# Edge stages: encoding, node rows and score products of the first two batches in the staggered order of the loop

## What is computed

```
x = x + gnn0(layernorm(x), src, dst, edge_attr)
x = x + ffn0(layernorm(x))          # top 2 of 8 experts
x = x + gnn1(layernorm(x), src, dst)
x = x + ffn1(layernorm(x))          # top 1 of 8 experts, with a capacity
```

```
alpha = sum(h[src]*a_src) + sum(h[dst]*a_dst) + sum(relu(edge_attr @ edge_W.T + edge_b) * h[dst])
alpha = leaky_relu(alpha, 0.2)
attn  = exp(alpha - segment_max(alpha)[dst]) / segment_sum(...)[dst]
out   = segment_sum(h[src] * attn, dst) + bias
```

## Time and profile before

| | us |
|---|---|
| median of 3 runs | 6731.35 |
| the profiled execution | 6730.72 |
| its span, first to last instruction | 6728.6 |
| busy in the span: TensorE | 4888.9 |
| GpSimd | 3649.6 |
| VectorE | 3264.7 |
| ScalarE | 1365.0 |

### The profile page before, as it was taken

How to read it: one execution, slowest core, us unless ns; L and a number is a source line. 1 busy time by engine, 2 the same in 40 slices (tenths; PEclk the granted TensorE clock), 3 DMA queues, 4 the chain that set the end, 5 groups by cost and what they waited for, 6 DMA issues and landing times. The chain is left out here.

```text
span 6728.6 us, 99218 instructions
## 1 busy us (share of the span) xinstructions
PE 4888.9 (73%) x19729; PEld 3527.3 (52%) x19729; DVE 3264.7 (49%) x5938; ACT 1365.0 (20%) x2977; POOL 3649.6 (54%) x3708
## 2 busy tenths in 40 slices
PE   1689999999999992359999625656565655643698
PEld 0245555555555551359999514444444444433698
DVE  6556666666666666311111324444454444445244
ACT  1322222222222220112222201111011111101122
POOL 1667777777777750332222067777777777711322
PEclk9899999999999996579999858888888888875899
DMA  6555555555555546146666555555555555533455
GB/s 218 178 137 157 153 153 155 156 153 156 154 154 155 156 117 216 42 147 181 181 183 186 155 127 142 139 139 139 139 141 138 143 136 142 138 99 120 163 199 190
DMA packets 718013, 1022.24 MB, mean 152 GB/s; under 512 B 301733, under 2 KB 531561, under 8 KB 692608
## 3 DMA queue, kind: packets, MB, share of 16 engines
q0 software_dynamic: 183456, 485.95, 27.7%
q1 hardware_dynamic: 527676, 519.31, 25.3%
q10 hardware_dynamic: 6564, 14.14, 0.6%
HBM read 868.26 MB, written 153.27 MB: 152 GB/s over the span
## 5 line engine op out<-in xcount | busy, mean ns | idle before, releaser
L773 POOL DMA_INDIRECT e_rows<-sc_table,e_eidx x3224 | 3152.7, 978 | 1140.3 <-issue 974.0
L872 PE MATMUL e_ps_o<-e_rows,e_oh 128*128 128x264 f32 x6448 | 1665.2, 403 | 288.8 <-ACT e_res L963 147.6
L872 PEld LDWEIGHTS e_ps_o<-e_rows,e_oh 128*128 128x128 f32 x6448 | 1214.2, 196 | 747.8 <-issue 573.1
L1126 DVE TENSOR_TENSOR e_rows<-e_rows,e_ps_w 128x1024 f32<-128x1024 f32 x806 | 970.2, 1206 | 7.8 <-ACT e_rows L956 3.5
L1058 DVE SCALAR_TENSOR_TENSOR e_u<-e_encr,e_adst,e_ps_hd 128x512 f32<-128x512 f32 x806 | 593.3, 744 | 659.2 <-PE e_ps_X L822 467.4
L822 PE MATMUL e_ps_X<-e_u,e_hwide 128*104 128x512 f32 x1612 | 812.7, 597 | 16.4 <-DVE e_u L1058 16.2
L963 ACT COPY e_res<-e_ps_o 32x264 f32<-32x264 f32 x806 | 296.2, 367 | 2483.5 <-PE e_ps_o L876 2057.7
L1670 PE MATMUL x_ps_h<-x_xT,x_w 128*128 128x256 f32 x2624 | 647.3, 405 | 13.9 <-DMA x_b<-in_L_ffn_b_dram 13.9
L1670 PEld LDWEIGHTS x_ps_h<-x_xT,x_w 128*128 128x128 f32 x2624 | 638.0, 337 | 18.6 <-issue 14.8
L1681 PE MATMUL x_ps_y<-x_w,x_hT 128*128 128x256 f32 x2624 | 579.9, 379 | 0.0
L936 ACT ACTIVATE e_encr<-e_ps_enc 128x512 f32<-128x512 f32 x806 | 475.9, 590 | 370.2 <-PE e_ps_enc L810 369.4
(11 more groups left out here) (290 smaller groups left out, 4057.6 us busy)
## 6 DMA issues: line engine op xcount, KB each, us to landing
x_w<-in_L_ffn_W_dram SPq DMA_DIRECT2D x112, 1024.0 KB
e_at<-sc_grp SPq DMA_DIRECT2D x403, 192.0 KB
x_w<-in_L_ffn_w_dram SPq DMA_DIRECT2D x60, 1024.0 KB
e_rows<-sc_table,e_eidx POOLq DMA_INDIRECT x3224
e_at<-sc_grp SPq DMA_DIRECT2D x403, 96.0 KB
sc_agg<-e_res SPq DMA_DIRECT2D x816, 33.0 KB
sc_xb<-r_zero SPq DMA_DIRECT2D x24, 1032.0 KB
x_xin<-sc_xb SPq DMA_DIRECT2D x86, 258.0 KB
```

The lines of the kernel that those rows point to most:

```text
L773: pool.indirect_dma_start(rows[:, k, s, j, :], None, dr["table"][:, :], bass.IndirectOffsetOnAxis(eidx[:, k, s, j:j + 1], 0)).then_inc(s_r ...
L872: nc.tensor.matmul(ps_o[:, 0:ROW], oh[:, k, at_j:at_j + P], rows[:, k, s, j, :], start=(j == 0), stop=False)
L1126: nc.vector.tensor_tensor(part, part, ps_w[:, k, :, s * HEADS:(s + 1) * HEADS].unsqueeze(3).to_broadcast([P, CH, HEADS, DH]), ALU.mult).th ...
```

## The change

On TensorE, `scores(b, s)` is replaced by `products(b)`, which goes through all 13 sub-batches of batch 0 or 1. In layer 0 it issues E(s,0), S(s-2,0), E(s,1), S(s-2,1), and the last four scores at the end; the wait for `u` ahead of a score goes, except for those last four (the encoding's own wait for `u` of s-1 covers it). In layer 1 it issues `score_owner(b, s-2)`, and the last two at the end. The wait for the score tile, `free_scores`, stands at s = 2. On VectorE the one-hot of s+1 is made before the products of s, not after them.

```
-            def scores(b, s):
-                if s == 0:
-                    free_scores(b)
-                if not first:
-                    score_owner(b, s)
-                    return
-                enc(b, s, 0)
-                enc(b, s, 1)
-                score(b, s, 0, True)
-                score(b, s, 1, True)
+            def products(b):
+                for s in range(SB):
+                    if s == 2:
+                        free_scores(b)
+                    if first:
+                        for h in range(2):
+                            enc(b, s, h)
+                            if s >= 2:
+                                score(b, s - 2, h, False)
+                    elif s >= 2:
+                        score_owner(b, s - 2)
+                if first:
+                    for s in range(SB - 2, SB):
+                        score(b, s, 0, True)
+                        score(b, s, 1, True)
+                else:
+                    score_owner(b, SB - 2)
+                    score_owner(b, SB - 1)
...
-            for s in range(SB):
-                scores(0, s)
+            products(0)
...
-            for s in range(SB):
-                scores(1, s)
+            products(1)
...
             for s in range(SB):
+                if s + 1 < SB:
+                    owners(0, 0, s + 1, (s + 1) % 2)
                 if first:
                     products(0, s, s % 2)
-                if s + 1 < SB:
-                    owners(0, 0, s + 1, (s + 1) % 2)
...
             for s in range(SB):
+                if s + 1 < SB:
+                    owners(1, 1, s + 1, (SB + s + 1) % 2)
                 if first:
                     products(1, s, (SB + s) % 2)
-                if s + 1 < SB:
-                    owners(1, 1, s + 1, (SB + s + 1) % 2)
```

## The result

The changed kernel takes 6696.77 us (median of 6 runs, 6693.58 to 6697.89); the kernel before, in 6 runs too, 6730.57 us. The ratio is 0.9951 [0.9938, 0.9964], a gain of 33.8 us. The forecast was 6697. The mechanism was right, but some of the terms were off by 2 to 4 us and cancel, so the hit to the microsecond is luck.

What follows compares the result with a forecast made beforehand. A TensorE chain bounds batches 0 and 1, GpSimd's gathers second; TensorE bounds the loop. Gain 35.6 at batch 1's logits less 1.8 for the clock is 33.8 us: 6696.9 from the profiled 6730.72, plus 0.6 for the median, 6697; range 6690 to 6711.

Steps and rivals of the forecast that it cites:

- The cycle: Layer 0, batches 0 and 1: a staggered sub-batch takes 2.58 us, set by TensorE, against 4.52; ReLU and VectorE stay under.
- A cold start of 7.4 us: Start of batches 0 and 1: TensorE's clock rises 7.4 us after the first matmul; a batch takes 38.4 us.
- The gathers end batch 0: Batch 0's logits wait for the 52nd gather, at 313.26 instead of 327.24: 13.98 us earlier.
- the 6.3 us of cover: Batch 0: TensorE's scores end 6.3 us ahead of need, as the logits wait for gathers.
- A slowdown of the gathers: Denser VectorE work could slow GpSimd's gather issue; taken as nothing, upper end 5 us at 1.30 per gather.
- Gather 104 and logits(1): Batch 1's logits wait for its last gather until 378.6, not 414.17; gain 35.6 us, TensorE standing still 4.2.
- The clock after that wait: After TensorE's 4.2 us stall at batch 1's logits, half clock costs 3.7 us or nothing; middle of 1.8 taken.
- Loads: VectorE's new wait for the next group's load has 1.1 us of slack; cost taken as nothing, DMA share about 0.75.
- rival 1: Loads pace the sub-batches of batches 0 and 1 at 3.4 us; gain 28.1, time 6703; 14%.
- Batch 2: GpSimd restarts at 376.3, 31.9 us earlier; its 52nd gather fits by 1.0 us; 0 to 3 may be lost, none taken.
- rival 2: The loop gives back 15 to 20 us through TensorE waits for gathers; 10 to 20 stay, time 6711 to 6721; 7%.
- Rivals 3 and 4: Batches 0 and 1: clock stays at half, 6747 us, 3%; or an overlooked wait keeps the 4.5 us cycle, 6731, 3%.

Runs made afterwards that it cites:

- the busier start: Changed kernel plus one extra 400-column matmul after each encoding of sub-batches 0 and 1 in batches 0 and 1 of layer 0; 7840.15 us, one run.
- the replaced gathers: Changed kernel with layer 0's gathers of batches 0 and 1 replaced by plain copies of the table's first rows; 6709.52 against 6735.45 us, 0.996.
- the run meant to part the two: Changed kernel with VectorE's one-hots of batch 0 held back until the gathered logits are copied; 7844.19 against 7875.9 us, 0.9962.

## Why the prediction was right, step by step

**The cycle**, forecast 2.58: 2.65. Of the other bounds that the step had listed, ReLU and VectorE's work stayed under it. The 0.07 comes to 0.8 us over eleven sub-batches; its cause isn't shown.

**A cold start of 7.4 us**: mis-sized. The step took the time to the rise from before, where TensorE's first sub-batches had scores in them. Staggered, sub-batches 0 and 1 have none, and the clock rose after 11.7 and 9.6 us, about 276.5 and 338.0. That is some 2 and 1 us per batch; the busier start, in its one run, and the rises of the other traces point to the sparse work. Forecast 38.4 per batch, measured 41.3 and 40.9.

**The gathers end batch 0**: right in kind, and the 6.3 us of cover took in batch 0's longer run. The 52nd was due at 307.71 less the 1.1 of the stage's start, 306.6, and came at 308.22: one issue took 2.41 us instead of 0.95. It stands beside VectorE's 1.89 us `e_oh`, as in five more kernels here. In the kernel before, the gather beside `e_oh` was the 67th, so it cost the logits of batch 0 nothing. A slowdown of the gathers, a term put at nothing, was thus 1.6 us. Nor is `e_oh` alone in this: the longest issue among batch 1's gathers lies beside a scan, which also reads two operands from SBUF, the memory of the engines. The timeline of the kernel after:

```profile
315.55 1.23 DVE L1090 TENSOR_TENSOR_SCAN e_fmax<-e_fr,e_lk 104x512 f32<-104x512 bf16 x1
...
315.72 1.80 POOL L773 DMA_INDIRECT e_rows<-sc_table,e_eidx  x1 [0.30 <-issue]
```

All six issues among the changed kernel's 104 that took over 1.06 us began while a VectorE operation of that kind ran, as the six long ones of the kernel before did. Then 2.94 to the copy and 0.68 to TensorE, as forecast. The delay that the forecast had weighed, by the Trainium skill's rule on tensor_scalar (SBUF — State Buffer, Who interferes with whom), would have come from the owner compares: the gathers beside these took at most 1.06 us, so the trace doesn't bear it out for them. Batch 1 begins 12.3 us earlier against the stage's start; the forecast had 13.98.

**Gather 104 and logits(1)**: against the stage's start the gather came 1.7 us later than before, the long issue again, and the copy came 3.98 us after it, not 2.87. The window 376 to 378 has a DMA share of 0.83 at 195 GB/s; that this traffic is the reason isn't shown. TensorE, itself 3.1 us later at the first aggregation than forecast, waited 2.83 (1.07 of it usual), not 4.2 more than usual. Forecast 378.6, measured 380.28, 33.9 earlier than before and 32.8 against the stage's start, where the forecast had 35.6.

**The clock after that wait**: of the two ends, the costly one. It fell at about 379 and was back at about 385.7, some 6.8 us at half speed, of which TensorE worked 5.4; eight aggregation matmuls took 3.73 us instead of 1.94. That is about 2.7 us where the middle of 1.8 stood, and the trace agrees with the Trainium skill's rule (TensorE: Matmul & The Clock Gate, HAM oscillation) there, though the wait was shorter than forecast. The period from the copy of batch 1 to that of batch 2 is 72.5 us, against 69.9: 2.6 us lost. But the forecast had looked only at gaps of that size and counted one fall. The trace of before has 16 more in the loop, each around the once-a-batch logits with their usual wait of 1.07 us. The timeline and the window of before at one of them:

```profile
699.79 1.82 PE L844 MATMUL e_ps_X<-e_ident,e_alog 128*104 128x128 f32 x8 [1.07 <-ACT e_alog L940]
701.41 2.93 PE L872 MATMUL e_ps_o<-e_rows,e_oh 128*128 128x264 f32 x8
```

```profile
700.00:702.00 2.00, 2.00 (x10) 1.90 (x10) 0.34 (x1) 0.26 (x1) 1.57 (x2) 0.50 0.60 121
```

**Loads and rival 1**: 0.65 us, once, where nothing was taken. VectorE waited for a load twice ahead of the first encoding and twice in batch 1, where one half of a sub-batch took 352.73 - 350.77 = 1.96 us instead of 1.30. With the cycle's 0.8 and the start's 1.1 this makes up batch 1's 40.9. DMA share rose to 0.69, not 0.75. It takes the crowd of the replaced gathers to make the rival come true.

**Batch 2 and rival 2**: GpSimd restarts at 376.87, its 32 us gap gone, and ScalarE's copy at 452.07 waits for no gather. No stall was added in the loop. The loop in fact ended 35.0 us early where it began 31.3 early. The clock accounts for it. Once a batch, at its logits, lies a seam where TensorE waits for ScalarE's copy. At the 28 seams of batches 2 to 29 it waits the same 1.07 us in both kernels, but the clock falls at only some of them, each time for 3.4 us: at 16 in the profile of before, at 14 in that of the changed kernel. From copy to copy a batch with such a fall takes 72.1 to 72.9 us, one without mostly 70.7 to 71.1 (the last batch apart). Two falls fewer are about 3.4 us. Why they were fewer isn't shown; in the other kernels profiled on chips of the 6730 kind there were 13 to 17.

**Rivals 3 and 4** fell for the whole change. Rival 3's mechanism is real: half of the change, at the same work, fell to it.

**The sum.** 35.6 - 1.8 was forecast. In the profile logits(1) came 33.9 earlier, the clock took it to 31.3, and the loop gave back 3.7, to 35.0; the 1.1 us from ahead of the stage are in each. So the mechanism, both bounds and the place where the gain stops were forecast rightly. That the time came out at 6697 is luck: logits(1) fell 2.8 us short against the stage's start, the clock behind it cost 0.8 more than taken, and the loop returned 3.7 that nobody had forecast.

## What to carry to other kernels

When an in-order engine stands between a producer and its own late consumer, issue the consumer one or two steps later, and give the engine that feeds it the same order: either half alone gained nothing that could be measured here. Then ask which stream is behind the chain that was shortened: here it was the gathers, and starting them 5.5 us earlier, in both layers, was worth 12 us more. A wait of 2.3 to 3.0 us in TensorE's stream cost twice in each of the three kernels that had one at logits(1), once as a wait and once in 6.8 us of half clock.

## What the runs showed of the hardware

- An indirect gather's issue of 0.95 us took 2.41, 2.41, 1.96, 1.96, 2.38 and 1.63 us when it lay beside the one-hot multiply-compare on VectorE (two operands from SBUF, 1.89 us), in six kernels; 1.73 in the kernel before. In the changed kernel it took 1.80 and 1.30 beside scans and 1.34 and 1.43 beside elementwise operations that also read two operands from SBUF. Owner compares (a tensor_scalar, 0.38 us) did nothing of the kind to the gathers beside them. The pairing is shown by position; the run meant to part the two fell on a chip where it could not.
- In the run with TensorE's order alone, TensorE had a hole of 1.60 us in each sub-batch and stayed at the lower level of 1.2 GHz for the first 36 us of batch 0; in batch 1, with the same holes, it reached 2.4 GHz after 12.5 us. Without the holes, in the changed kernel, it took 11.7 and 9.6 us, and 4.8 to 7.4 us in the old order.
- In a stream in which TensorE is busy 69 of 72 us the clock fell for 3.4 us at 16 of 28 seams before and at 14 after, each time around a wait of 1.07 us. Behind waits of 2.83, 3.04 and 2.26 us, in three kernels, it fell for 6.8 us.
- On two of the chips a kernel that takes 6730 us elsewhere takes 7759 and 7876. While the gathers ran, TensorE, ScalarE and VectorE advanced one sub-batch per 21 to 23 us, with no cause named in the records. It wasn't found.
